# Order of the five steps in three packed 16-head attentions: the step of the left-over query rows goes from fourth to last

## What is computed

```
scores = einsum('bhqd,bhkd->bhqk', q, k) * 0.25      (masked as above)
probs  = softmax(scores, axis=-1)
ctx    = einsum('bhqk,bhkd->bqhd', probs, v)          then a 256x256 output projection
```

## Time and profile before

| | |
|---|---|
| median of 3 runs | 742.25 us (735.38 to 744.55) |
| the profiled execution's own time | 738.47 us |
| its span on the core | 736.7 us |
| PE busy | 670.8 us, 91% of the span |
| PEld, DVE, ACT, POOL busy | 507.3, 418.1, 244.1, 265.9 us |
| mean granted clock of TensorE | 0.984 |

### The profile page before, as it was taken

How to read it: one execution, slowest core, us unless ns; L and a number is a source line. 1 busy time by engine, 2 the same in 40 slices (tenths; PEclk the granted TensorE clock), 3 DMA queues, 4 the chain that set the end, 5 groups by cost and what they waited for, 6 DMA issues and landing times. The chain is left out here.

```text
span 736.7 us, 18989 instructions
## 1 busy us (share of the span) xinstructions
PE 670.8 (91%) x7243; PEld 507.3 (69%) x7243; DVE 418.1 (57%) x1084; ACT 244.1 (33%) x583; POOL 265.9 (36%) x301
## 2 busy tenths in 40 slices
PE   7899789799999789989998889889999899889997
PEld 5677689544446668845486777776436678889996
DVE  4839567777772466667536465736782665612211
ACT  2046301256663042135515310514563162112110
POOL 2459041445653130134217135500552402243121
PEclk9999999999999999999999999999999999989999
DMA  9603069545551468656323091202463133937503
GB/s 349 269 1 75 4 248 388 180 126 157 162 152 60 131 197 358 258 168 214 111 81 75 9 394 40 39 3 80 158 213 127 38 35 136 361 98 279 185 20 117
DMA packets 53212, 112.25 MB, mean 152 GB/s; under 512 B 20163, under 2 KB 33668, under 8 KB 50180
## 3 DMA queue, kind: packets, MB, share of 16 engines
q1 hardware_dynamic: 42562, 88.50, 34.9%
q0 software_dynamic: 6144, 15.21, 6.8%
q10 hardware_dynamic: 4418, 7.33, 2.8%
HBM read 96.79 MB, written 14.23 MB: 151 GB/s over the span
## 5 line engine op out<-in xcount | busy, mean ns | idle before, releaser
L287 PE MATMUL ps<-const_sb 128*128 128x128 f32 x1146 | 148.3, 285 | 7.4 <-DMA const_sb<-in_consts 4.2
L287 PEld LDWEIGHTS ps<-const_sb 128*128 128x128 f32 x1146 | 140.6, 199 | 13.0 <-issue 7.7
L2308 PE MATMUL ps<-l_w,const_sb 128*32 (+1 forms) x236 | 97.8, 544 | 5.1 <-DMA l1e_own_gu<-in_l_experts 2.0
L2308 PEld LDWEIGHTS ps<-l_w,const_sb 128*32 128x32 f32 (+1 forms) x236 | 27.3, 121 | 47.3 <-issue 42.7
L2350 PE MATMUL ps<-l_w,row_sb 128*32 (+1 forms) x214 | 55.6, 387 | 0.5 <-ACT row_sb L2424 0.5
L315 POOL TENSOR_TENSOR norm_r<-norm_ve,const_sb 128x2 f32<-128x2 f32 (+1 forms) x27 | 19.5, 724 | 97.2 <-DVE norm_ve L308 68.1
L2308 PE MATMUL ps<-w_sb,const_sb 128*64 128x512 f32 x104 | 49.0, 594 | 0.0
L423 ACT ACTIVATE x_fm<-ps 128x256 f32<-128x256 f32 x35 | 12.2, 382 | 107.6 <-PE ps L396 107.6
L2216 POOL DMA_INDIRECT l0e_y_scratch<-row_sb,l0e_rows_u x26 | 27.6, 1061 | 35.1 <-ACT row_sb L2443 34.8
L2328 PEld LDWEIGHTS ps<-const_sb 128*128 128x128 f32 x117 | 12.1, 142 | 35.9 <-issue 19.0
L2350 PEld LDWEIGHTS ps<-l_w,row_sb 128*32 128x32 f32 (+1 forms) x214 | 22.5, 122 | 18.6 <-issue 9.0
(11 more groups left out here) (553 smaller groups left out, 1543.5 us busy)
## 6 DMA issues: line engine op xcount, KB each, us to landing
l_w<-in_l_experts SPq DMA_DIRECT2D x1, 8704.0 KB, 27.0
l_w<-in_l_experts SPq DMA_DIRECT2D x1, 8192.0 KB, 23.4
expert_w<-in_l_experts SPq DMA_DIRECT2D x4, 2048.0 KB, 8.2
l_more_w<-in_l_experts SPq DMA_DIRECT2D x4, 2048.0 KB, 9.0
l1e_own_gu<-in_l_experts SPq DMA_DIRECT2D x11, 704.0 KB
w_sb<-in_l_biases SPq DMA_DIRECT2D x52, 128.0 KB, 3.1
l_w<-in_l_experts SPq DMA_DIRECT2D x1, 6144.0 KB, 20.1
l2e_own_gu<-in_l_experts SPq DMA_DIRECT2D x11, 512.0 KB, 3.6
```

Source lines behind the costliest of these rows:

```text
L287: pe.matmul(ps[:, bank, 0:P], ident, ident, start=True, stop=True)
L2308: mm = pe.matmul(to[c * R:(c + 1) * R, :], xg_fm[:, r % 2, k, c * R:(c + 1) * R], own_gu[:, c - 1, r % 2, c0:c0 + wide] if c else whole(wh ...
```

## The change

`REST` becomes 4, so that the order is bunch 0, 1, 2, 3, left rows; `bunch(n)` is not needed any more and goes. In `pe_steps` the left rows' value products stand in one piece, behind the contexts of bunch 3 and ahead of those of the left rows; bunch 3's value products take the place that other bunches' have. The three unused matmuls between the last two contexts go. DVE's and ACT's code is not edited beyond `bunch(e)`; it follows `REST`.

```diff
-            STEPS, REST = BUNCHES + 1, BUNCHES - 1
+            STEPS, REST = BUNCHES + 1, BUNCHES
...
-            def bunch(n):
-
-                return n if n < REST else n - 1
-
...
-                for n in range(1, STEPS + 2):
+                for n in range(1, STEPS + 3):
                     if scored <= n < STEPS:
                         stay_awake(pe, ahead[n], 7)
                         pe_scores(pe, n)
-                    if n == STEPS:
-
-                        pe.wait_ge(s_read, STEPS)
-                        pe.wait_ge(s_pfm, 2 * REST + 2)
-                        rest_values(pe, range(0, BLOCKS // 2))
                     if 0 <= n - 1 < STEPS:
                         e = n - 1
...
                         mm.then_inc(s_pt, 1)
-                    if n == STEPS:
-                        rest_values(pe, range(BLOCKS // 2, BLOCKS)).then_inc(s_av, 1)
-                    if 0 <= n - 3 < REST:
+                    if 0 <= n - 3:
                         pe_contexts(pe, n - 3)
-                    if 0 <= n - 2 < STEPS and n - 2 != REST:
+                    if n - 2 == REST:
+
+                        pe.wait_ge(s_read, STEPS)
+                        pe.wait_ge(s_pfm, 2 * REST + 2)
+                        rest_values(pe, range(BLOCKS)).then_inc(s_av, 1)
+                    if 0 <= n - 2 < REST:
                         e = n - 2
                         pe.wait_ge(s_pfm, 2 * e + 2)
                         if e == 0:
                             pe.wait_ge(s_placed, 2 * 16 * REP)
                         if e >= 1:
 
-                            pe.wait_ge(s_ctx, min(e, REST))
+                            pe.wait_ge(s_ctx, e)
...
                         mm.then_inc(s_av, 1)
-                pe_contexts(pe, REST)
-                stay_awake(pe, 3)
-                pe_contexts(pe, STEPS - 1)
                 stay_awake(pe, 4)
```

More of the change, by code:

```diff
@@ L863, in act_steps @@
                         if e != REST:
-                            dst = ctx_fm[:, :, BUNCH * bunch(e) * SEQ:BUNCH * (bunch(e) + 1) * SEQ]
+                            dst = ctx_fm[:, :, BUNCH * e * SEQ:BUNCH * (e + 1) * SEQ]
                             act.activation(dst.rearrange("p k (c j) -> p k c j", c=4)[:, :, :, 0:WIDE],
@@ L877, in pe_scores @@
                 if n != REST:
[L878 to L882, removed]
+                    if upto(by_pool, n):
+                        pe.wait_ge(s_kbd, upto(by_pool, n))
+                    if upto(by_dve, n):
+                        pe.wait_ge(s_kbd_v, upto(by_dve, n))
+                    by_now = len([own for own in by_act if own[0] <= n])
                     if by_now:
@@ L885, in pe_scores @@
                     for name in QUERIES:
-                        made(pe, name, bunch(n) // 2)
+                        made(pe, name, n // 2)
                 else:
@@ L899, in pe_scores @@
                             for c in range(4):
-                                b = 4 * c + i if n == REST else BUNCH * bunch(n) + c
+                                b = 4 * c + i if n == REST else BUNCH * n + c
                                 q = stationary(q_left[:, m, k, :], b) if n == REST \
@@ L981, in pe_steps @@
                                                p_fm[0:rows, e % 2, g, 32 * c:32 * c + 32],
-                                               v_bd[0:rows, BUNCH * bunch(e) + c, 0:NR[g], g, :], start=True, stop=True)
+                                               v_bd[0:rows, BUNCH * e + c, 0:NR[g], g, :], start=True, stop=True)
                         mm.then_inc(s_av, 1)
-                pe_contexts(pe, REST)
-                stay_awake(pe, 3)
-                pe_contexts(pe, STEPS - 1)
                 stay_awake(pe, 4)
```

## The result

The changed kernel takes 745.98 us (median of 11 runs, 742.87 to 751.58) against 741.24 us (11 runs, 735.38 to 744.55) of the kernel before. The ratio is 1.0086, 95% interval 1.0059 to 1.0112: slower by 6.4 us, between 4.4 and 8.3. (The two medians alone are 4.7 us apart; the ratio is not their quotient.) The forecast was 744.8 us, 2.5 above the kernel before, and within 2%. The direction, the 2% and the range held; the size was less than half of what the ratio gives.

A forecast was written before the change was run, and what follows sets the result against it. PE was taken to be bound by instruction supply, in blocks of about 127 matmuls. Layer 0 +1.4, layer 2 +1.4, latent +0.2 and tail -0.5 sum to +2.5 us, on 742.25 giving 744.8 us; range 737 to 750.

The forecast's parts named there:

- The rival without such stalls (-5.0 us): All three attentions: instruction supply doesn't hold PE, or holds it elsewhere, so the change is faster, 737.2 us; chance 0.2.
- the count: All three attentions: block boundaries stay at their old places in PE's instruction count; layer 0's at 52, 179, 306, 432, 558, 685.
- The first effect: Last bunch's scores are ready early: in layer 0 DVE's softmax of step 3 starts at about 77.0 us, not 81.61.
- The second: Blocks stay where they are in the count: layer 0's last transposes start at 89.05 us, before 89.62.
- record 179 is reached when its block is there: Layer 0, 59 into the left scores: PE reaches this block boundary at 80.1 us without having to wait.
- pass 132 unhindered: Latent attention: left scores start at 474.0 us, cross this block boundary without a stall and end at 475.95.
- The third effect: Behind the last transposes: left value products stall at a block boundary; layer 0's last contexts at 97.7 us against 96.29.
- The tail: Last contexts to projection: at full clock 0.4 and 0.7 us come back in layer 2 and latent; half taken, -0.5.
- The clock's (+7.5): Attention tails: new gaps bring the lower clock, at most 1.65 us each, +5.0 on top, 749.8 us; chance 0.12.
- the three signs of being wrong: No stall in the left value products, blocks not 127 records apart, or a tail's clock 0.50 from ahead of those products.
- the third rival: All attentions: ends are set block after block in both orders, gains and losses cancel: 0, 742.3 us; chance 0.18.

The follow-up runs named there:

- the repetition: The changed kernel once more, unedited, beside the kernel before on the same chip: 746.88 us against 740.05, ratio 1.0124; its trace is of an execution of 743.08 us.

## Why the prediction was right, and where its size was off

*What bounds these stretches.* Right. Where two blocks in a row stall, the stalls stand 126 to 128 matmuls and 3.3 to 4.0 us apart, in every trace, and moving them by a few instructions without any change to an attention's code took most of the loss away. The rival without such stalls (-5.0 us) has nothing for it.

*The places.* In layer 0 the boundary was forecast three to five matmuls ahead of the end of the left value products, and it is three. In the latent attention 17 were forecast and it is five; in layer 2's it was forecast at 95 of 192 and is at 99. The step that failed is the count: it took the old place of the boundaries over, while each earlier attention has six records less now. Twelve less by the third attention are just the difference of 17 and 5. In layer 2's the stall of 0.65 us is 0.50, and absent in the repetition.

The sum can be laid beside both traces of the changed kernel. The first one's span is 13.1 us longer than before and the repetition's 4.6, near the 4.7 to 6.8 of the medians; in the latter these stretches hold all of the difference:

| us | before | forecast | first trace | repetition |
|---|---|---|---|---|
| layer 0: fourth step's scores to last transposes | 14.62 | 14.05 | 15.59 | 14.76 |
| layer 0: from there to last contexts | 6.67 | 8.65 | 8.94 | 8.84 |
| layer 2: fourth step's scores to last transposes | 9.04 | 9.8 | 9.38 | 9.54 |
| layer 2: from there to last contexts | 6.48 | 7.15 | 6.74 | 6.21 |
| latent: fourth step's scores to last transposes | 8.95 | 8.35 | 9.79 | 10.17 |
| latent: from there to last contexts | 7.94 | 8.75 | 9.08 | 8.26 |
| all three: last contexts to the end of the projection | 19.6 | 19.1 | 24.3 | 20.2 |
| sum | 73.3 | 75.9 | 83.8 | 78.0 |

*The first effect* was right: bunch 3's softmax starts 1.93 us behind its scores (77.94), where the left rows', which stood in this place before, started 81.61-75.00 = 6.6 us behind theirs. *The second* was mis-sized: from the step's scores to the last transposes I had 14.05 us in layer 0 and 8.35 in the latent attention, where the trace has 91.60-76.01 = 15.6 (14.8 in the repetition) and 9.8 (10.2). The term "record 179 is reached when its block is there" failed: the block had been asked for late, and came at 82.27, 6.3 us behind the start, not 5.0. So did the latent attention's "pass 132 unhindered": its left scores stall for 0.75 us (1.13). In the repetition this is the largest miss of the sum, 1.8 us. That a block is asked for as soon as the one before it is entered was the assumption behind both. For layer 2's 9.8 were forecast and 9.4 measured.

*The third effect*, from the last transposes to the last contexts: forecast 8.65, 7.15 and 8.75 us, measured 8.94, 6.74 and 9.08. This part of the sum holds within half a microsecond in this trace and within one in the repetition. In layer 0 it does so by luck: the lower clock stretched the left value products from 2.2 to 3.84 us in both traces, and the stall of 2.2 us that had been reckoned is 0.44 and 0.20.

*The tail.* In the first trace this is the term that failed most. I had -0.5 us, from tails that might run at full clock. In the profiled pair the way from last contexts to the projection grew by 1.1 us in layer 0 and 0.4 in the latent attention and fell by 0.4 in layer 2's, and the projections behind layer 0 and the latent attention took 1.6 and 2.0 us longer, a place that the sum did not hold at all. In the repetition only the latter is left: 6.23 us for 4.55. Over the runs, 0.004 to 0.008 less of mean clock, at 5.5 to 6.7 us for 0.01, would be 2 to 5 us, if the clock were what makes the runs of one kernel differ. That was not tried apart, and the kernel before without the three unused matmuls ahead of its last contexts speaks against so plain a reckoning: 0.0045 less of clock, and no time lost that could be measured.

*The rivals.* The clock's (+7.5) came nearer to the measured 6.4 than the forecast did, and its mechanism was there: of the three signs of being wrong that the prediction names, the last one, a clock of 0.50 from ahead of the left value products, stands in layer 0 in both traces (from 92.8 and 90.5 us). But it was put as an alternative to the stalls, and both are there. Over the runs, moving the boundaries brought the clock back (0.9795) and the time with it, while filling the gaps brought the clock back (0.980) and left 4.3 to 6.7 us. What lets the clock fall differs by place. In the latent attention it falls behind the stall, so that this with the wait for the division is likely the cause. In layer 0 it falls ahead of that stall, behind the wait for the exponential, also in the two kernels whose left value products have no stall (from 92.8 and 93.6 us), and not where the gaps are filled (99.7). How the loss divides between the stalls and the clock was not shown. No effect, the third rival, is excluded by both intervals.

## What to carry to other kernels

Where small matmuls are unrolled as densely as here, look for PE's instruction supply as the bound: count instructions from one stall by "issue" to the next, and look at which instruction each boundary hits. A boundary just ahead of the last instruction that another engine waits for cost the stall plus that engine's work (2.47+0.82 us in the latent attention); a few instructions less far ahead hid the one beside the other. So measure a reordering at more than one such offset before it is judged. Unused matmuls that keep the clock up are instructions too: six of them less in each attention of the kernel before were worth 0.35 and 0.54%. And a lower mean clock is a reason to look, not a price.

## What was not expected of the hardware

- The packet for the next block came 1.1 us behind a boundary in dense stretches (80.04 to 81.18 us before), and 3.1 us behind it where PE waited for ACT shortly behind the boundary (76.8 to 79.9 us; 2.6 us in the repetition).
- Three unused matmuls less at the start of the program moved the ratio from 1.0086 and 1.0124 to 1.0013.
- The lower clock lasted for 13.6 us in layer 0 with PE busy for 11.24 of them by the modelled ends of its matmuls (the first row of the stretches above).
- The kernel before without the three unused matmuls ahead of its last contexts ran at a mean clock of 0.9745 against 0.979, and no time was lost that could be measured (1.0000, 0.9970 to 1.0031).
